# Self-attention values multiplied by high and low parts, with a triangle of value differences

## The chip, the cores and the metric

The program runs on one core of one Trainium2 chip. Its engines are TensorE (PE; its weight loads are the rows PEld), VectorE (DVE), ScalarE (ACT), GpSimd (POOL) and SyncE (SP), which starts most DMAs. Each engine works through its own queue of instructions in order and waits on semaphores. The metric is the device time of one launch in microseconds; less is better. Before the change it is 1614.92 us, the median of 3 runs (1614.67 to 1617.2).

## What is computed

One decoder layer on x of 4 x 512 x 512 in float32: a self-attention, a cross-attention, and a feed-forward with ternary weights. Only the self-attention and one side job of it (the mean of the absolute feed-forward weights) are touched:

```python
q = h @ wq_comp @ wq_up                       # 16 heads of 128
q = _rmsnorm(_apply_partial_rope(q, cos, sin), q_norm_w)
k = _rmsnorm(_apply_partial_rope(h @ wk, cos, sin), k_norm_w)
v = h @ wv                                    # one k and one v for all heads
mask = (diff >= 0) & (diff < WIN)             # WIN = 128, diff = query - key
probs = jax.nn.softmax(jnp.concatenate([scores, sink], axis=-1), axis=-1)
attn = jnp.einsum('bhts,bsd->bhtd', probs[..., :t], v)
...
scale = 1.0 / jnp.clip(jnp.mean(jnp.abs(w)), EPS)   # of each feed-forward weight
```

## The kernel before

The self-attention (phase_self_attention) takes the tokens in 16 tiles of 128 rows and the 16 heads in 4 groups of 4, so that there are 64 steps, step k being tile k // 4 and group k % 4. The window of 128 keys means that a query row sees keys of its own tile up to itself, and the keys behind them in the tile before. The first tile of each batch of four has its own tile only. The text calls its steps one-block steps (k = 0 to 3, 16 to 19, 32 to 35, 48 to 51) and the 48 others two-block steps.

A row of probabilities has just 128 live keys over both tiles. So copy_predicated (L547) lays the scores of both tiles over one another in 128 columns, the softmax runs on 128 columns, and the transposed probabilities ps_pT are parted again by two multiplications with 0/1 triangles: pT_own (L572) with the triangle of the own tile, pT_prev (L575) with the other. Two float32 matmuls, L729 and L732, multiply them with the values of the own tile and the tile before and add up in ps_a. Nearly all other matmuls of the phase are made by the helper three (L659 to L662): each operand is split into a high part rounded to float32r and a low part, and hi x hi, hi x lo and lo x hi are added up. The split costs one ACT copy (the high part) and one DVE subtraction (the low part).

The engines are software-pipelined by hand. In loop round c each engine does, in the order of its code:
- PE: scores of step c, values of step c - 2 (ps_a), transposition of q of step c + 1 (L742), transposition of the probabilities of step c - 1 (L754), up-projection of step c + 3, now and then work on a new tile (transposition of h when c % 4 is 1, the k/v/q projection when c % 4 is 2, transposition of k when c % 4 is 0), and the output product of step c - 3 (12 matmuls).
- DVE: copy_predicated and maximum of step c, neg_max (L553), aT_lo of c - 2, neg_r (L563), qT_lo of c + 1, pT_own and pT_prev of c - 1, the sum q_ss of c + 2, f_part (L585, the sum of absolute feed-forward weights, in rounds 0 to 23) and at the end inv_den of step c, the reciprocal at L602.
- ACT: aT_hi of c - 2 (L447), qT_hi of c + 1 (L451), the four exponentials of step c (L458), sink_exp (L461), the quantisation of a feed-forward chunk (L442 and L467, rounds 24 to 47), h (L474, when c % 4 is 0), and the copy q of c + 3 (L481). qcT_hi and kT_hi (L431, L434) of a new tile stand at the start of rounds with c % 4 of 1.
- POOL: squares and rotary embedding of q of step c + 2 (L629 and rotate, L613 to L617), the same for k of a new tile when c % 4 is 3, sink_arg (L643), den (L647), the multiplication of the probabilities by inv_den (L650), and q_r of c + 2 (L655).

PE may start the scores of c + 1 only when the exponentials of step c have read ps_s. There is no planner: the code's order is the order of the queues.

## Time and profile before

| | before |
|---|---|
| median of 3 runs | 1614.92 us (1614.67 to 1617.2) |
| the profiled execution, its own time | 1617.68 us |
| its span, first to last instruction | 1615.8 us |
| PE busy | 1549.0 us, 96% |
| DVE, ACT, POOL busy | 1228.1, 1186.8, 1267.7 us |
| self-attention steps | about 73 us to 588 us |

The profiled execution lies 2.8 us above the median. The page gives busy time for each engine, and the span in 40 slices of 40.4 us with the busy share in tenths; self-attention ends in the 15th slice. The granted TensorE clock is 1.00 throughout from 120 to 560 us. The columns of a timeline row are start, duration, engine, line, operation, output and inputs, and in brackets the engine's idle time before it and what ended it. Rows overlap where the next instruction starts before the last has ended, so the cost of one in a chain is the distance of two starts.

### The profile page before, as it was taken

What the parts mean: (1) busy time and instruction counts of PE and PEld (TensorE: products, weight loads), DVE (VectorE), ACT (ScalarE), POOL (GpSimd) and SP (SyncE); (2) the same over time, 40 slices, a digit from 0 to 9 for tenths busy, and PEclk for the clock granted to TensorE, in tenths of its full rate; (3) what the DMA queues carried; (4) which work ended last, traced back from release to release, by engine and by line L of the source; (5) the groups of instructions that cost most, each with busy time, mean ns of one, the idle gap of its engine ahead of it and who ended that gap; (6) DMA issues with size and microseconds to landing.
All of it is one profiled execution on the core that took longest, in us unless ns stands there. A gap on an engine that the chain in (4) does not pass through costs nothing. (4 is left out here: it accounts for less than half of the span.)

```text
span 1615.8 us, 23949 instructions
## 1 busy us (share of the span) xinstructions
PE 1549.0 (96%) x7520; PEld 1072.6 (66%) x7520; DVE 1228.1 (76%) x2242; ACT 1186.8 (73%) x1962; POOL 1267.7 (78%) x1141
## 2 busy tenths in 40 slices
PE   8999999999999988999999999999999978999996
PEld 3577787787788756666666666766666536666664
DVE  2489989878877756788978888788888666767773
ACT  2454556778755435999999889989998937878875
POOL 0487787787787724999999999999999949988850
...
DMA packets 57191, 110.24 MB, mean 68 GB/s; under 512 B 9245, under 2 KB 13597, under 8 KB 56683
## 3 DMA queue, kind: packets, MB, share of 16 engines
...
q8 instruction: 62, 1.02, 0.3%
q10 hardware_dynamic: 1578, 1.07, 0.2%
...
## 5 line engine op out<-in xcount | busy, mean ns | idle before, releaser
L1443 POOL TENSOR_TENSOR x_p_lo<-x_p,x_p_hi 128x1024 fp32r<-128x1024 f32 x255 | 603.0, 2397 | 59.3 <-ACT x_p_hi L1209 34.4
L1345 DVE TENSOR_REDUCE x_maxes<-x_ps_a 128x1 f32<-128x1024 f32 x252 | 306.9, 1218 | 114.4 <-PE x_ps_a L1544 110.7
L1172 ACT ACTIVATE x_p<-x_ps_b,x_any_valid 128x1024 f32<-128x1024 f32 x256 | 284.8, 1113 | 55.8 <-PE x_ps_b L1524 49.7
L1209 ACT ACTIVATE x_p_hi<-x_p 128x1024 fp32r<-128x1024 f32 x256 | 271.2, 1060 | 6.3
L1524 PE MATMUL x_ps_b<-x_Q,x_K 103*128 103x512 f32 x512 | 218.9, 509 | 12.1 <-ACT x_p L1172 10.0
L1584 PE MATMUL x_ps_o<-x_p_hi,x_V 128*96 128x512 f32 x512 | 208.6, 407 | 2.7 <-POOL x_p_lo L1443 2.1
L1585 PE MATMUL x_ps_o<-x_p_lo,x_V 128*96 128x512 f32 x512 | 201.3, 393 | 0.0
L1544 PE MATMUL x_ps_a<-x_K,x_Q 99*128 99x512 f32 x504 | 164.5, 407 | 4.7 <-POOL x_Q L1431 2.8
L1524 PEld LDWEIGHTS x_ps_b<-x_Q,x_K 103*128 103x128 f32 x512 | 87.5, 191 | 106.3 <-issue 58.8
L447 ACT ACTIVATE a_aT_hi<-a_ps_a 128x512 fp32r<-128x512 f32 x64 | 38.3, 598 | 153.8 <-PE a_ps_a L732 124.2
L458 ACT ACTIVATE a_work<-a_ps_s,a_neg_max,a_q_r 128x128 f32<-128x128 f32 x256 | 113.9, 464 | 7.9 <-DVE a_neg_max L553 7.7
L1544 PEld LDWEIGHTS x_ps_a<-x_K,x_Q 99*128 99x128 f32 x504 | 90.5, 190 | 40.4 <-DVE x_maxes L1345 16.5
L650 POOL TENSOR_TENSOR a_work<-a_work,a_inv_den 128x512 f32<-128x512 f32 x64 | 67.7, 1057 | 58.7 <-DVE a_inv_den L602 58.7
L1584 PEld LDWEIGHTS x_ps_o<-x_p_hi,x_V 128*96 128x96 f32 x512 | 82.7, 161 | 43.5 <-POOL x_p_lo L1443 5.4
L660 PE MATMUL a_ps_out<-a_w_hi,a_aT_hi 128*128 128x512 f32 x256 | 104.5, 408 | 0.0
L1585 PEld LDWEIGHTS x_ps_o<-x_p_lo,x_V 128*96 128x96 f32 x512 | 83.0, 162 | 30.2
L661 PE MATMUL a_ps_out<-a_w_lo,a_aT_hi 128*128 128x512 f32 x256 | 101.3, 396 | 0.0
L662 PE MATMUL a_ps_out<-a_w_hi,a_aT_lo 128*128 128x512 f32 x256 | 101.1, 395 | 0.0
L629 POOL TENSOR_TENSOR a_work<-a_q 128x512 f32<-128x512 f32 x64 | 66.4, 1037 | 16.0 <-ACT a_q L481 16.0
L661 PE MATMUL a_ps_s<-a_kT_lo,a_qT_hi 128*128 128x256 f32 (+1 forms) x256 | 72.3, 282 | 0.0
L662 PE MATMUL a_ps_s<-a_kT_hi,a_qT_lo 128*128 128x256 f32 (+1 forms) x256 | 72.0, 281 | 0.0
L1984 PE MATMUL f_ps_u<-shared,f_hqT 128*128 128x512 bf16 x256 | 67.3, 386 | 4.6 <-DVE f_f L1928 4.6
...
## 6 DMA issues: line engine op xcount, KB each, us to landing
...
```

Source lines behind the costliest of these rows:

```text
L458: act.activation(p[:, c % 2, j, :], ps_s[:, j, 0:P], ACT.Exp, scale=q_r[:, c % 4, j:j + 1], bias=neg_max[:, c % 2, j:j + 1], accum_out=row ...
L660: pe.matmul(out_ap, hi, rhs_hi, start=start, stop=False)
L661: pe.matmul(out_ap, hi, rhs_lo, start=False, stop=False)
L662: return pe.matmul(out_ap, lo, rhs_hi, start=False, stop=stop)
L1172: act.activation(p[:, v % 3, :, :], ps_b[:, :, :], ACT.Exp, scale=any_valid[:, b % 2:b % 2 + 1]).then_inc(exp_ready, 1)
L1209: act.activation(p_hi[:, r], p[:, v % 3], ACT.Copy).then_inc(hi_ready, 1)
L1345: dve.tensor_reduce(out=maxes[:, c % 2, 3 + r:4 + r], in_=scores_bank(n)[:, :, :], axis=mybir.AxisListType.XY, op=ALU.max).then_inc(max_re ...
L1443: pool.tensor_tensor(out=p_lo[:, v % 3, blocks], in0=p[:, v % 3, blocks], in1=p_hi[:, r, blocks].bitcast(F32), op=ALU.subtract)\
L1524: last = pe.matmul(ps_b[:, j, :], K[0:ROWS + 7, g, kb * P:(kb + 1) * P], Q[0:ROWS + 7, hh, :], start=True, stop=True)
L1544: last = pe.matmul(scores_bank(n)[:, j, :], Q[0:ROWS + 3, h2, r * P:(r + 1) * P], K[0:ROWS + 3, g2, j * 512:(j + 1) * 512], start=True, st ...
L1584: pe.matmul(bank[0:ROWS, :], vs, p_hi[:, rw, j], start=(rw == 0 and j == 0), stop=False)
L1585: last = pe.matmul(bank[0:ROWS, :], vs, p_lo[:, w % 3, j], start=False, stop=(rw == 3 and j == 1))
```

## The change

The values v, and the difference dv of the values of the tile before and the own tile, are split into high and low parts. The probabilities ps_pT are no longer masked for the own tile: all of them are multiplied with the own tile's v, and the part of the other triangle is multiplied with dv = v(before) - v(own), which corrects it. Both products are done by three, so each step has 3 or 6 float32r matmuls where it had 1 or 2 float32 ones.

For this ACT makes pT_hi (a copy, ahead of the exponentials of the same round), DVE makes pT_lo, pT_prev_hi and pT_prev_lo (3 instructions where 2 were; pT_own is gone), and per tile ACT makes v_hi and dv_hi, POOL dv, v_lo and dv_lo. On DVE the three stand behind the sum q_ss and just ahead of the reciprocal; pT_own and pT_prev stood ahead of q_ss. The sum of absolute weights f_part moves from DVE (tensor_reduce) to ACT (Abs with an accumulated output), in the same rounds.

```diff
         def _(act):
...
+                if 0 <= c - 1 < STEPS:
+                    k = c - 1
+                    act.wait_ge(pT_made, k + 1)
+                    if k:
+                        act.wait_ge(a_made, k)
+                    act.activation(pT_hi[:, :], ps_pT[:, :], ACT.Copy).then_inc(pT_hi_ready, 1)
                 if 0 <= c < STEPS:
                     act.wait_ge(neg_max_ready, 4 * c + 4)
...
+                t = tile_of(c, 1)
+                if t is not None:
+                    act.wait_ge(v_ready, t + 1)
+                    if t >= 2:
+                        act.wait_ge(a_made, 4 * (t - 1))
+                    act.activation(v_hi[:, t % 2, :], v[:, t % 3, :], ACT.Copy).then_inc(v_hi_ready, 1)
+                t = tile_of(c, 0)
+                if t is not None and t % TPB:
+                    act.wait_ge(dv_ready, two_block_tiles(t + 1))
+                    act.activation(dv_hi[:, t % 2, :], dv[:, :], ACT.Copy).then_inc(dv_hi_ready, 1)
+                if 0 <= c < FFN_CHUNKS:
+                    act.wait_ge(f_abs_in[c % 4], 16 * (c // 4 + 1))
+                    act.activation(f_abs[:, c % 4, :], f_abs[:, c % 4, :], ACT.Abs, accum_out=f_part[:, c:c + 1]).then_inc(f_part_ready, 1)
...
         def _(dve):
...
-                    dve.tensor_tensor(out=pT_own[:, :].rearrange("p (a b) -> p a b", a=G1), in0=ps_pT[:, :].rearrange("p (a b) -> p a b", a=G1),
-                                      in1=own_part, op=ALU.mult).then_inc(pT_own_ready, 1)
-                    if len(blocks(k // 4)) == 2:
-                        dve.tensor_tensor(out=pT_prev[:, :].rearrange("p (a b) -> p a b", a=G1), in0=ps_pT[:, :].rearrange("p (a b) -> p a b", a=G1),
-                                          in1=prev_part, op=ALU.mult).then_inc(pT_prev_ready, 1)
...
-                    if 0 <= c < FFN_CHUNKS:
-                        dve.wait_ge(f_abs_in[c % 4], 16 * (c // 4 + 1))
-                        dve.tensor_reduce(out=f_part[:, c:c + 1], in_=f_abs[:, c % 4, :], axis=AXX, op=ALU.add,
-                                          apply_absolute_value=True).then_inc(f_part_ready, 1)
...
+                    dve.wait_ge(pT_hi_ready, k + 1)
+                    if k:
+                        dve.wait_ge(a_made, k)
+                    dve.tensor_tensor(out=pT_lo[:, :], in0=ps_pT[:, :], in1=pT_hi[:, :].bitcast(F32), op=ALU.subtract).then_inc(pT_lo_ready, 1)
+                    if len(blocks(k // 4)) == 2:
+                        dve.tensor_tensor(out=pT_prev_hi[:, :].rearrange("p (a b) -> p a b", a=G1), in0=ps_pT[:, :].rearrange("p (a b) -> p a b", a=G1),
+                                          in1=prev_part, op=ALU.mult).then_inc(pT_prev_hi_ready, 1)
+                        dve.wait_ge(pT_lo_ready, k + 1)
+                        dve.tensor_tensor(out=pT_prev_lo[:, :].rearrange("p (a b) -> p a b", a=G1),
+                                          in0=pT_lo[:, :].bitcast(F32).rearrange("p (a b) -> p a b", a=G1),
+                                          in1=prev_part, op=ALU.mult).then_inc(pT_prev_lo_ready, 1)
                 if 0 <= c < STEPS:
                     dve.wait_ge(den_ready, c + 1)
...
         def _(pool):
...
+                t = tile_of(c, 1)
+                if t is not None:
+                    if t % TPB:
+                        pool.wait_ge(v_ready, t + 1)
+                        if two_block_tiles(t):
+                            pool.wait_ge(dv_lo_ready, two_block_tiles(t))
+                        pool.tensor_tensor(out=dv[:, :], in0=v[:, (t - 1) % 3, :], in1=v[:, t % 3, :], op=ALU.subtract).then_inc(dv_ready, 1)
+                    pool.wait_ge(v_hi_ready, t + 1)
...
+                t = tile_of(c, 0)
+                if t is not None and t % TPB:
+                    pool.wait_ge(dv_hi_ready, two_block_tiles(t + 1))
...
         def _(pe):
...
-                    last = pe.matmul(ps_a[:, :], v[:, blk[-1], :], pT_own[:, :], start=True, stop=len(blk) == 1)
+                    if k % 4 == 0:
+                        pe.wait_ge(v_lo_ready, t + 1)
+                    last = three(ps_a[:, :], v_hi[:, t % 2, :], v_lo[:, t % 2, :], pT_hi[:, :], pT_lo[:, :], True, len(blk) == 1)
                     if len(blk) == 2:
...
-                        last = pe.matmul(ps_a[:, :], v[:, blk[0], :], pT_prev[:, :], start=False, stop=True)
+                        pe.wait_ge(pT_prev_lo_ready, two_blocks(k + 1))
+                        last = three(ps_a[:, :], dv_hi[:, t % 2, :], dv_lo[:, t % 2, :], pT_prev_hi[:, :], pT_prev_lo[:, :], False, True)
```

v shrinks from four tiles to a ring of three (in the buffer work), so ACT's copy into it (L420) waits for v_lo of two tiles back and the last dv instead of for the products.

The order on DVE in a two-block round of a later tile, before, from neg_max to the reciprocal:

```order
L553 TENSOR_SCALAR a_neg_max<-a_s_max,a_neg_r,a_neg_sinks 128x1 x4
L558 TENSOR_TENSOR a_aT_lo<-a_ps_a,a_aT_hi 128x512
L563 TENSOR_SCALAR a_neg_r<-a_q_r 128x4
L565 TENSOR_TENSOR a_qT_lo<-a_ps_qT,a_qT_hi 128x512
L572 TENSOR_TENSOR a_pT_own<-a_ps_pT,a_window 128x512
L575 TENSOR_TENSOR a_pT_prev<-a_ps_pT,a_window 128x512
L580 TENSOR_REDUCE a_q_ss<-a_work 128x4
L582 TENSOR_SCALAR a_q_ss<-a_q_ss 128x4
L602 RECIPROCAL a_inv_den<-a_den 128x4
```

The same place of the changed kernel (its line numbers are larger):

```order
L587 TENSOR_SCALAR a_neg_max<-a_s_max,a_neg_r,a_neg_sinks 128x1 x4
L592 TENSOR_TENSOR a_aT_lo<-a_ps_a,a_aT_hi 128x512
L597 TENSOR_SCALAR a_neg_r<-a_q_r 128x4
L599 TENSOR_TENSOR a_qT_lo<-a_ps_qT,a_qT_hi 128x512
L604 TENSOR_REDUCE a_q_ss<-a_work 128x4
L606 TENSOR_SCALAR a_q_ss<-a_q_ss 128x4
L625 TENSOR_TENSOR a_pT_lo<-a_ps_pT,a_pT_hi 128x512
L627 TENSOR_TENSOR a_pT_prev_hi<-a_ps_pT,a_window 128x512
L630 TENSOR_TENSOR a_pT_prev_lo<-a_pT_lo,a_window 128x512
L635 RECIPROCAL a_inv_den<-a_den 128x4
```

The work on the transposed probabilities went behind the sum and has one instruction more, and the reciprocal stays last.

The order on ACT from the exponentials of a round with c % 4 of 0 (c = 12, while the feed-forward weights are summed) to kT_hi of the next round, before:

```order
L458 ACTIVATE a_work,a_row_sum<-a_ps_s,a_neg_max,a_q_r 128x128 x4
L461 ACTIVATE a_sink_exp<-a_sink_arg 128x4
L474 ACTIVATE shared<-a_xt,a_ln_bias,a_ln_rstd 128x512
L481 ACTIVATE a_q<-a_ps_up 128x512
L431 ACTIVATE a_qcT_hi<-a_ps_front 128x128
L434 ACTIVATE a_kT_hi<-a_ps_front 128x128
```

The same place of the changed kernel, from pT_hi:

```order
L472 ACTIVATE a_pT_hi<-a_ps_pT 128x512
L479 ACTIVATE a_work,a_row_sum<-a_ps_s,a_neg_max,a_q_r 128x128 x4
L482 ACTIVATE a_sink_exp<-a_sink_arg 128x4
L492 ACTIVATE a_dv_hi<-a_work 128x128
L495 ACTIVATE shared,a_f_part<-shared 128x1024
L508 ACTIVATE shared<-a_xt,a_ln_bias,a_ln_rstd 128x512
L515 ACTIVATE a_q<-a_ps_up 128x512
L446 ACTIVATE a_qcT_hi<-a_ps_front 128x128
L449 ACTIVATE a_kT_hi<-a_ps_front 128x128
```

dv_hi and the sum of absolute weights now stand between sink_exp and kT_hi, and pT_hi stands ahead of the exponentials.

## Rows read from the trace of the kernel before

**Rows 1.** The page: busy time of the engines, and their tenths in 40 slices

```profile
PE 1549.0 (96%) x7520; PEld 1072.6 (66%) x7520; DVE 1228.1 (76%) x2242; ACT 1186.8 (73%) x1962; POOL 1267.7 (78%) x1141
...
PE   8999999999999988999999999999999978999996
```

**Rows 2.** Stretches of the self-attention: busy time by engine, granted clock, DMA share

```profile
120.00:260.00 140.00, 140.00 (x756) 112.45 (x755) 129.16 (x302) 73.14 (x252) 110.25 (x190) 1.00 0.35 81
260.00:460.00 200.00, 200.00 (x1079) 159.68 (x1078) 168.76 (x423) 151.58 (x398) 161.81 (x271) 1.00 0.36 106
```

**Rows 3.** PE timeline of round 59 (two blocks), then of round 34 (one block)

```profile
541.85 1.02 PE L729 MATMUL a_ps_a<-a_pT_own,a_v 128*128 128x512 f32 x2
542.71 1.02 PE L732 MATMUL a_ps_a<-a_pT_prev,a_v 128*128 128x512 f32 x2
543.57 0.60 PE L742 MATMUL a_ps_qT<-ident,a_q 128*128 128x128 f32 x4
544.01 0.60 PE L754 MATMUL a_ps_pT<-ident,a_work 128*128 128x128 f32 x4
544.36 0.48 PE L660 MATMUL a_ps_up<-a_up_hi,a_qcT_hi 128*128 128x512 f32 x1
...
545.38 0.39 PE L661 MATMUL a_ps_out<-a_w_lo,a_aT_hi 128*128 128x512 f32 x1
545.61 0.39 PE L662 MATMUL a_ps_out<-a_w_hi,a_aT_lo 128*128 128x512 f32 x1
...
343.70 1.07 PE L729 MATMUL a_ps_a<-a_pT_own,a_v 128*128 128x512 f32 x2
344.61 0.60 PE L742 MATMUL a_ps_qT<-ident,a_q 128*128 128x128 f32 x4
```

**Rows 4.** DVE timeline: the reciprocals of rounds 18, 22, 34, 38 and 42

```profile
221.02 0.17 DVE L602 RECIPROCAL a_inv_den<-a_den 128x4 f32<-128x4 f32 x1
...
253.23 0.16 DVE L602 RECIPROCAL a_inv_den<-a_den 128x4 f32<-128x4 f32 x1
...
348.69 0.17 DVE L602 RECIPROCAL a_inv_den<-a_den 128x4 f32<-128x4 f32 x1
...
379.66 0.17 DVE L602 RECIPROCAL a_inv_den<-a_den 128x4 f32<-128x4 f32 x1
...
412.44 0.17 DVE L602 RECIPROCAL a_inv_den<-a_den 128x4 f32<-128x4 f32 x1
```

**Rows 5.** Who waited for whom, whole phase: us in total, times, longest

```profile
POOL a_work L650 <- DVE a_inv_den L602: 58.7, 64, 2.6
...
ACT a_sink_exp L461 <- POOL a_sink_arg L643: 33.5, 32, 2.6
```

**Rows 6.** ACT and DVE timelines from round 44 into round 45

```profile
428.06 1.17 ACT L467 ACTIVATE shared<-shared,a_f_clip 128x1024 bf16<-128x1024 f32 x1
429.10 0.83 ACT L474 ACTIVATE shared<-a_xt,a_ln_bias,a_ln_rstd 128x512 f32<-128x512 f32 x1
...
435.62 0.23 ACT L458 ACTIVATION_READ_ACCUMULATOR a_work<-a_ps_s,a_neg_max,a_q_r 128x1 f32 x1
...
430.78 0.29 DVE L528 TENSOR_TENSOR a_qcT_lo<-a_ps_front,a_qcT_hi 128x128 fp32r<-128x128 f32 x1 [1.03 <-ACT a_kT_hi L434]
```

**Rows 7.** Groups of instructions by form: busy us, mean ns, idle before

```profile
L585 DVE TENSOR_REDUCE a_f_part<-shared 128x1 f32<-128x1024 f32 x24 | 29.0, 1210 | 0.0
...
L575 DVE TENSOR_TENSOR a_pT_prev<-a_ps_pT,a_window 128x512 f32<-128x512 f32 x48 | 32.5, 677 | 0.0
...
L614 POOL TENSOR_TENSOR a_q_t<-a_q,a_rope 128x128 f32<-128x128 f32 x64 | 29.4, 459 | 0.0
...
L451 ACT ACTIVATE a_qT_hi<-a_ps_qT 128x512 fp32r<-128x512 f32 x64 | 38.0, 593 | 2.4 <-PE a_ps_qT L742 2.4
```

**Rows 8.** Two lines of DVE by themselves (min/median/max ns), and POOL beside the second

```profile
L563 DVE TENSOR_SCALAR a_neg_r<-a_q_r x64: 158/279/742, 69.9 to 566.9; 128x4 f32<-128x4 f32 x64
...
1286.61 3.78 DVE L1373 TENSOR_TENSOR x_p_lo<-x_p,x_p_hi 128x1024 fp32r<-128x1024 f32 x1 [7.53 <-ACT x_p_hi L1209]
...
1284.60 4.71 POOL L1443 TENSOR_TENSOR x_p_lo<-x_p,x_p_hi 128x1024 fp32r<-128x1024 f32 x2
```

More of the change, by code:

```diff
@@ L194, in phase_self_attention @@
         kT_lo = sb("kT_lo", [P, TPB * P], F32R)
[L195 removed]
+        v_hi = sb("v_hi", [P, 2, P], F32R)
+        v_lo = sb("v_lo", [P, 2, P], F32R)
+        dv_hi = sb("dv_hi", [P, 2, P], F32R)
+        dv_lo = sb("dv_lo", [P, 2, P], F32R)
         q = sb("q", [P, 2, G1, P])
[L197 removed]
         q_ss = sb("q_ss", [P, 2, G1])
```

47 lines of the change are left out of this document (29 added, 18 removed).

## Prediction

> **What bounds the kernel now.** I read the page first: PE is busy 96% of the span and at 9 tenths in nearly every slice of the self-attention [rows 1]. The stretches say the same more sharply: from 120 to 460 us PE has no idle time at all, at a granted clock of 1.00 [rows 2]. So PE sets the pace of the rounds, and shorter PE work shortens them, until something else does. The same rows show that the something else is near: DVE is busy 129.16 of 140 us up to 260 us, and POOL 161.81 of 200 after it. POOL's idle time, moreover, is mostly waiting: 58.7 us for the reciprocal in 64 rounds, and ACT waited for POOL's sink_arg in 32 of them [rows 5]. That is a ring, POOL to ACT to POOL to DVE to POOL. I therefore price the change twice, on PE, and on that ring.
>
> **The change on PE.** A float32 value matmul costs 0.86 us from start to start (541.85 to 542.71, 542.71 to 543.57), 0.91 in a one-block round (343.70 to 344.61) [rows 3]. A float32r matmul of 512 columns costs 0.23 (545.38 to 545.61), so three cost 0.70. The transposition behind the values takes 0.44 (543.57 to 544.01), and the next one, which does not follow a float32 product, 0.35 [rows 3]; I take 0.08 of that as gained too. A two-block round thus gains 2 x 0.16 + 0.08 = 0.40 us, a one-block round 0.16 to 0.21 + 0.08, say 0.25. Sum: 48 x 0.40 + 16 x 0.25 = 23.2 us, if nothing else binds; without the 0.08 it is 18. The worst bound is that no float32r matmul overlaps the next, as the single duration of 0.39 [rows 3] would have it, which loses 0.3 per product; the start-to-start distances speak against it.
>
> **The change on the ring.** Follow it over four rounds, from the reciprocal of one round with c % 4 of 2 to that of the next. The reciprocal releases POOL's multiplication; POOL then works without a gap through q_r, the squares, the rotation and, at c % 4 of 3, k's rotation, to sink_arg; ACT's sink_exp, den and the reciprocal follow, then POOL's round again up to sink_exp of c % 4 = 0. Then ACT has to get through its tail to kT_hi, for which DVE sat idle 1.03 us even before [rows 6], and DVE runs two rounds nearly without idling. Before, these four rounds took 253.23 - 221.02 = 32.2 us and 379.66 - 348.69 = 31.0 us where the one-block rounds had let PE run fast, that is, where the ring decided; where PE decided they took 412.44 - 379.66 = 32.8 [rows 4]. The change moves PE's 32.8 to 32.8 - 4 x 0.40 = 31.2. On the ring it adds:
> - POOL: dv and v_lo, 128x128 each like L614, 0.46 us busy and some 0.42 start to start: +0.84 [rows 7]. dv_lo runs beside DVE's rounds and is hidden by them.
> - ACT: dv_hi, +0.2 (a quarter of the columns of L451's 0.59, bounds 0.15 and 0.3) [rows 7]. In rounds 0 to 23 also the absolute sum: ACT's pass over 128x1024 is 1.04 from start to start (428.06 to 429.10) [rows 6], with an accumulator read 1.15.
> - DVE, in each of its two rounds: 3 instructions for 2 of 0.60 (0.677 busy) [rows 7], +0.6, so +1.2. In rounds 0 to 23 f_part's 1.21 [rows 7] goes, 1.13 start to start, in those two rounds and some 0.9 of it ahead of the third reciprocal: -3.2.
> - The port of POOL. pT_prev_lo is the first DVE operation of this phase's rounds with both large inputs in SBUF. What one costs beside POOL is seen at 1286.61: 3.78 us for 128x1024, ending when POOL's two had ended and its own pass was done [rows 8]. The tiny L563 takes 158 to 742 ns for the same 4 columns [rows 8], long when POOL is in the middle of an instruction. So I price pT_prev_lo from 0.6 (nobody in the way) to 0.6 + 1.0 (a whole L650 to wait for), and POOL's next instruction from 0 to 0.6 late. It mostly runs while POOL waits for the reciprocal behind it, where it costs POOL nothing; at c % 4 of 3 or 0 POOL is late and they meet. I take +0.6 per four rounds.
>
> By the Trainium skill, page "SBUF — State Buffer", section "Who interferes with whom", a DVE instruction with two SBUF inputs and a POOL instruction that reads SBUF exclude each other for the whole of the first one. The trace agrees with it in the 3.78 us of [rows 8]; by it all 48 pT_prev_lo could meet POOL, which is the slower rival below.
>
> The ring sums to: up to round 24, 32.2 + 0.84 + 0.2 + 1.15 - 3.2 + 1.2 + 0.6 = 33.0; in rounds 25 to 47, 31.0 + 0.84 + 0.2 + 1.2 + 0.6 = 33.8; behind them, without the quantisation's 1.04 on ACT and 0.4 on DVE, about 32.2. Compare with PE's 32.8 before and 31.2 after: in most of the phase the ring binds, and takes the gain.
>
> **What hides, and what the ring may be late by.** pT_hi (0.48 start to start) on ACT stands ahead of the exponentials, but values and transpositions come 0.3 earlier; the next scores start at 437.60, 1.8 us after the exponentials of round 45 ended (435.62 + 0.23) [rows 6], and 0.4 + 0.2 of that goes. So the ring can be some 1.2 us late before PE feels it, and 1.9 more behind one-block rounds, whose DVE work lacks copy_predicated and two pT instructions. The accumulation of f_part on ACT can wait for the same loads as before; the loads lead by two rounds and add nothing. The waits for v's ring of three are for work of a round or more ago: 0. No table load is added for Abs in the order of the program.
>
> **The sum by stretches** (after minus before; rounds counted from one c % 4 = 2 to the next):
> - ramp, rounds 0 to 5: DVE loses f_part, which the first rounds wait for; -1.0.
> - rounds 6 to 25: five groups, 33.0 against 32.8 in the two-block ones, the first with 1 us of slack in hand, one-block ones 0.6 better: -1.1.
> - rounds 26 to 49: 3 groups at 33.8 - 32.9 = +0.9, the one-block pair +0.2 and +0.7, the last, half without quantisation, -0.9: +2.7.
> - rounds 50 to 63: PE's pace again, 14 rounds at 0.25 to 0.40, with a little lost at 54: -4.6.
>
> Together -4.0. The profiled execution's 1617.68 becomes 1613.7; against the median, 2.8 lower, **1611**. Nothing behind the phase changes; what is gained ahead of its end carries over one to one.
>
> **Rivals.**
> 1. PE keeps the pace. If POOL and DVE absorb the additions (dv and v_lo under the reciprocal's wait of 0.9 us per round [rows 5], pT_prev_lo never meeting POOL), most of 23 us comes: -13 to -23, so 1592 to 1602. For it: POOL idles 38 of 200 us and DVE 31 [rows 2]. Against it: the ring's 31.0 and 32.2 us.
> 2. The port decides and the time ends slower. If pT_prev_lo meets POOL in every two-block round, DVE waits 0.4 (half of an average POOL instruction) in its two rounds on the ring and POOL 0.6 in its two: +2.0 per group in place of +0.6. Nine groups with 1.4 more each is +12.6: 1611 + 12 = 1623. It decides from the point where the ring exceeds PE's old 32.8, which it does already.
> 3. The float32r products don't gain (0.28 to 0.30 each beside fresh weights): PE is then unchanged, and the additions hide less: 1615 to 1618.
>
> **How the numbers follow.** Chances: my forecast, 1605 to 1616, 0.42; PE's pace, 0.28; the port, 1617 to 1630, 0.23; no gain on PE, 0.07. The likeliest case's own range is 1605 to 1616. For 8 in 10 the range reaches from 1594 into rival 1 to 1622 into rival 2. About 0.2% (3.2 us) is what a measurement of this kernel can tell from no change. Faster by more (under 1611.7): 0.28 + 0.21 of my case = 0.49. Within it: 0.21 + 0.06 = 0.27. Slower: 0.24.
>
> **What would show it.** On PE: value triples at 0.70 and rounds of 7.13 us behind round 56, in any case. Rounds 36 to 47: PE idle ahead of the scores, released by ACT's exponentials, or ahead of the up-projection, released by kT_lo, near c % 4 of 1 and 2; without such idling rival 1 has it. pT_prev_lo: a median near 0.68 with a tail to 1.3; a median near 1 is rival 2. Reciprocals four rounds apart: 33.8. I am wrong on the ring if these read 31.2, and on DVE if the reciprocal no longer ends POOL's waits. PE's idling could also lower the granted clock, which was 1.00 here [rows 2]; that would add to the slow side.

## The result, and the profile after the change

The changed kernel takes 1623.83 us (median of five runs, 1619.61 to 1624.43). The ratio to the kernel before is 1.0040, with a 95% interval of 1.0025 to 1.0054: slower by 0.4%, where 0.25% faster was forecast, and the time lies above the range of 1594 to 1622. The 1614.92 us from which the prediction started is at the low end for the kernel before: beside the experiments its medians were 1616.6 to 1617.6 us. So the ratios below, each with the 95% interval, say more than differences of medians taken at different times.

Busy time of the engines, from the page of the changed kernel, against [rows 1]:

```profile
PE 1535.3 (95%) x7599; PEld 1087.2 (67%) x7632; DVE 1235.5 (76%) x2266; ACT 1249.0 (77%) x2102; POOL 1293.4 (80%) x1181
```

PE has 14 us less work than before, DVE 7 more, ACT 62 more and POOL 26 more. What that does shows in the stretches of the self-attention, in the columns of [rows 2], with one more stretch behind them:

```profile
120.00:260.00 140.00, 136.45 (x777) 116.17 (x777) 117.74 (x293) 98.50 (x305) 113.78 (x194) 1.00 0.32 81
260.00:460.00 200.00, 193.15 (x1093) 162.82 (x1092) 177.75 (x433) 163.93 (x432) 166.64 (x278) 1.00 0.35 105
460.00:560.00 100.00, 99.50 (x573) 85.16 (x572) 84.22 (x206) 61.09 (x201) 85.69 (x144) 1.00 0.17 59
```

Before, PE was busy for the whole of both stretches; now it idles 3.6 and 6.9 us in them. PE itself became faster, as forecast in kind. Its timeline in round 58:

```profile
539.62 0.39 PE L708 MATMUL a_ps_a<-a_pT_hi,a_v_hi 128*128 128x512 f32 x1
539.86 0.39 PE L709 MATMUL a_ps_a<-a_pT_lo,a_v_hi 128*128 128x512 f32 x1
540.09 0.40 PE L710 MATMUL a_ps_a<-a_pT_hi,a_v_lo 128*128 128x512 f32 x1
540.79 0.47 PE L708 MATMUL a_ps_a<-a_pT_prev_hi,a_dv_hi 128*128 128x512 f32 x1 [0.30 <-DVE a_pT_prev_lo L630]
541.10 0.39 PE L709 MATMUL a_ps_a<-a_pT_prev_lo,a_dv_hi 128*128 128x512 f32 x1
541.33 0.40 PE L710 MATMUL a_ps_a<-a_pT_prev_hi,a_dv_lo 128*128 128x512 f32 x1
541.57 0.60 PE L795 MATMUL a_ps_qT<-ident,a_q 128*128 128x128 f32 x4
542.00 0.60 PE L807 MATMUL a_ps_pT<-ident,a_work 128*128 128x128 f32 x4
```

A product of three float32r matmuls takes 0.70 (539.62 + 3 x 0.23) where the float32 one took 0.86 [rows 3]; the second one here takes 0.78, since its first matmul comes behind a wait. The transposition behind it still takes 0.43. The 0.30 in brackets is new: PE waits for the last part that DVE makes.

Who waits for whom in the self-attention (us in total, times, longest), against [rows 5]:

```profile
ACT a_sink_exp L482 <- POOL a_sink_arg L676: 71.9, 50, 3.0
ACT a_aT_hi L462 <- PE a_ps_a L710: 53.9, 35, 3.6
POOL a_work L683 <- DVE a_inv_den L635: 50.4, 64, 2.3
POOL a_den L680 <- ACT a_sink_exp L482: 27.5, 64, 1.9
DVE a_inv_den L635 <- POOL a_den L680: 23.6, 24, 2.1
DVE a_qcT_lo L562 <- ACT a_kT_hi L449: 18.6, 15, 2.3
...
PE a_ps_up L708 <- DVE a_kT_lo L565: 6.2, 9, 1.0
PE a_ps_pT L807 <- POOL a_work L683: 5.1, 10, 1.5
PE a_ps_s L763 <- ACT a_work L479: 3.6, 3, 2.3
```

ACT's wait for sink_arg has doubled (33.5 us in 32 rounds before), and DVE waits 23.6 us for POOL's den, ahead of the reciprocal, where it waited 4.1 us before. The last three rows are the largest waits of PE itself. One turn of the ring, at the end of round 43 (c % 4 of 3), on POOL, ACT and DVE:

```profile
426.95 0.32 POOL L646 TENSOR_TENSOR shared<-shared,a_rope 128x64 f32<-128x64 f32 x1
...
428.58 0.83 POOL L672 TENSOR_TENSOR shared<-shared,a_qk_w 128x128 f32<-128x128 f32 x1
429.38 0.20 POOL L676 TENSOR_TENSOR a_sink_arg<-a_neg_max,a_sinks 128x4 f32<-128x4 f32 x1
429.89 0.20 POOL L680 TENSOR_TENSOR a_den<-a_row_sum,a_sink_exp 128x4 f32<-128x4 f32 x1 [0.32 <-ACT a_sink_exp L482]
430.38 1.04 POOL L683 TENSOR_TENSOR a_work<-a_work,a_inv_den 128x512 f32<-128x512 f32 x1 [0.29 <-DVE a_inv_den L635]
```

```profile
426.67 0.21 ACT L479 ACTIVATION_READ_ACCUMULATOR a_work<-a_ps_s,a_neg_max,a_q_r 128x1 f32 x1
429.61 0.20 ACT L482 ACTIVATE a_sink_exp<-a_sink_arg 128x4 f32<-128x4 f32 x1 [2.73 <-POOL a_sink_arg L676]
429.72 0.29 ACT L488 ACTIVATE a_v_hi<-a_work 128x128 fp32r<-128x128 f32 x1
429.92 1.14 ACT L501 ACTIVATE shared<-shared,a_f_clip 128x1024 bf16<-128x1024 f32 x1
430.96 0.57 ACT L515 ACTIVATE a_q<-a_ps_up 128x512 f32<-128x512 f32 x1
```

```profile
430.12 0.18 DVE L635 RECIPROCAL a_inv_den<-a_den 128x4 f32<-128x4 f32 x1 [1.03 <-POOL a_den L680]
```

The exponentials end at 426.88. POOL is by then in the rotations of q and k and comes to sink_arg 2.5 us later; ACT idles 2.73 us, and its ReLU, its copy of q and all that follows are late by that.

Where the phase lost its time, by the start of the first score matmul of a round in the two profiled runs (after minus before): +0.1 us at round 6, +2.9 at 26, +6.4 at 50, +5.4 at 63. In the whole span the profiled runs differ by only 1.9 us, since the rest of the program had a higher granted clock in this run of the changed kernel (0.994 on average over the span, against 0.990); its other four runs took 1622.3 to 1624.4 us at 0.992. (The clock also differed inside the ramp, 0.93 before and 0.96 changed from 73 to 120 us; from 120 to 560 us it was 1.00 in both.) Against a kernel before of 1616.7 us the ratio of 1.0040 is 6.5 us, and the phase's 5.4 is most of it.

### The profile page after: what moved, and what is told of

Read it like the earlier page. It is cut to its first block and busy times, and to the rows that moved or that the text cites. A ratio compares the mean times of both kernels' runs of the same rounds, so it can differ in the third digit from the quotient of the medians.

```text
span 1617.8 us, 24457 instructions
## 1 busy us (share of the span) xinstructions
PE 1535.3 (95%) x7599; PEld 1087.2 (67%) x7632; DVE 1235.5 (76%) x2266; ACT 1249.0 (77%) x2102; POOL 1293.4 (80%) x1181
## 5 line engine op out<-in xcount | busy, mean ns | idle before, releaser
L708 PE MATMUL a_ps_s<-a_kT_hi,a_qT_hi 128*128 128x256 f32 (+1 forms) x256 | 72.0, 281 | 1.5 <-ACT a_work L479 1.5
```

The costliest lines, as they stand in the source:

```text
L708: pe.matmul(out_ap, hi, rhs_hi, start=start, stop=False)
```

## The experiments

All are edits of the changed kernel, but for the last. The ratio is to the kernel before; the changed kernel stands at 1.0040. Where an expectation names a value of c % 4 for ACT's or POOL's waits, it counts by the round that PE is in, one ahead of the instruction's own for the sink's exponential, den and the reciprocal.

### Does the ring bind, or PE?

**PE's products put back to float32**, nothing else changed:

```diff
-last = three(ps_a[:, :], v_hi[:, t % 2, :], v_lo[:, t % 2, :], pT_hi[:, :], pT_lo[:, :], True, len(blk) == 1)
+last = pe.matmul(ps_a[:, :], v_hi[:, t % 2, :].bitcast(F32), pT_hi[:, :].bitcast(F32), start=True, stop=len(blk) == 1)
```

> The changed kernel with its two float32r triples on PE put back as one float32 product each, v_hi x pT_hi and dv_hi x pT_prev_hi (the low parts are still made on all engines, but not used, so the result lacks their share). PE's round is as long as before the change, all other engines' work is that of the changed kernel. Theory 1 (the ring of POOL, ACT and DVE binds in rounds 6 to 49, where four rounds take 33.6 to 34.1 us against 32.9 of PE's old pace): only the rounds with PE's pace lose, 14 at the end x 0.33 and the ramp, so 1624 + 4 to 8 = 1628 to 1632. Theory 2 (PE still sets the pace and something else stalls it now and then): all 48 x 0.33 + 16 x 0.15 = 18 us come back, 1642.

Measured: 1627.52 us, ratio 1.0061 (1.0049 to 1.0073). That is half a microsecond below theory 1 and 14 below theory 2: in this kernel PE's saving is worth 0.2%, 3.4 us, and not 18. In rounds 26 to 49 the phase took 4.4 us more than before, against 3.5 in the changed kernel. The ring binds.

**All that was added beside PE taken out** (pT_prev_lo, dv, v_lo and dv_lo, and all but 8 columns of the absolute sum):

```diff
-in0=pT_lo[:, :].bitcast(F32).rearrange("p (a b) -> p a b", a=G1),
-in1=prev_part, op=ALU.mult).then_inc(pT_prev_lo_ready, 1)
...
-pool.tensor_tensor(out=dv[:, :], in0=v[:, (t - 1) % 3, :], in1=v[:, t % 3, :], op=ALU.subtract)
-pool.tensor_tensor(out=v_lo[:, t % 2, :], in0=v[:, t % 3, :], in1=v_hi[:, t % 2, :].bitcast(F32), op=ALU.subtract)
-pool.tensor_tensor(out=dv_lo[:, t % 2, :], in0=dv[:, :], in1=dv_hi[:, t % 2, :].bitcast(F32), op=ALU.subtract)
...
-act.activation(f_abs[:, c % 4, :], f_abs[:, c % 4, :], ACT.Abs, accum_out=f_part[:, c:c + 1])
+act.activation(f_abs[:, c % 4, 0:8], f_abs[:, c % 4, 0:8], ACT.Abs, accum_out=f_part[:, c:c + 1])
```

> The changed kernel without what it adds beside PE: no pT_prev_lo (PE uses pT_prev_hi in its place), no dv, v_lo and dv_lo on POOL (PE uses v_hi and dv_hi in their place, dv_hi is a copy of v), and the absolute sum over 8 of its 1024 columns; the result is not the reference's in these parts. PE's work is that of the changed kernel. Theory 1 (ring): PE's pace of 7.20 per two-block and 6.68 per one-block round in nearly all of the phase, so 16 to 20 us below the kernel before, 1595 to 1599. Rival (PE's product triples save less than the rows say, or the granted clock falls when PE idles less evenly): 1608 or more.

Measured: 1598.87 us, ratio 0.9885 (0.9873 to 0.9898). Here the whole saving arrives, and PE is busy without a gap again, in the stretches from 120 and from 260 us of this kernel:

```profile
120.00:260.00 140.00, 140.00 (x817) 122.17 (x816) 111.60 (x294) 88.17 (x319) 115.27 (x198) 1.00 0.34 81
260.00:460.00 200.00, 200.00 (x1166) 174.22 (x1165) 172.64 (x431) 168.85 (x449) 165.52 (x274) 1.00 0.35 106
```

Its two-block rounds without tile work take 7.21 us against 7.53, its one-block rounds 6.41 against 6.57: 0.32 and 0.16 per round. Four rounds take 31.6 us, against 32.9 before and 33.6 to 34.1 in the changed kernel.

### What each addition costs

**pT_prev_lo read from PSUM**, of the same size, but without a second large SBUF input:

```diff
-in0=pT_lo[:, :].bitcast(F32).rearrange("p (a b) -> p a b", a=G1),
+in0=ps_pT[:, :].rearrange("p (a b) -> p a b", a=G1),
```

> The changed kernel with pT_prev_lo made from ps_pT in PSUM instead of from pT_lo in SBUF (it holds a wrong part then, which falsifies the result a little); DVE has the same number of instructions of the same size, but none with two large SBUF inputs. Theory of the port (POOL's instructions that meet pT_prev_lo are stretched or held, some 1.4 us per group of four rounds over nine groups): 1611 to 1613. Theory of plain additions (the ring is late from the count of instructions; only two or three small POOL instructions per group are held 0.4 each): 1618 to 1622. If the port does nothing: 1623 to 1625.

Measured: 1616.08 us, ratio 0.9991 (0.9977 to 1.0005): a gain of 0.5%, between the theory of the port (1611 to 1613) and that of plain additions (1618 to 1622). The port costs that, but mostly not on DVE. By line (min/median/max ns), pT_prev_lo, sink_arg and den of the changed kernel:

```profile
L630 DVE TENSOR_TENSOR a_pT_prev_lo<-a_pT_lo,a_window x48: 672/676/989, 116.1 to 584.8; 128x512 fp32r<-128x512 f32 x48
L676 POOL TENSOR_TENSOR a_sink_arg<-a_neg_max,a_sinks x64: 188/199/654, 76.1 to 578.5; 128x4 f32<-128x4 f32 x64
L680 POOL TENSOR_TENSOR a_den<-a_row_sum,a_sink_exp x64: 198/200/664, 77.9 to 580.6; 128x4 f32<-128x4 f32 x64
```

and of this one:

```profile
L630 DVE TENSOR_TENSOR a_pT_prev_lo<-a_ps_pT,a_window x48: 671/675/684, 118.1 to 580.9; 128x512 fp32r<-128x512 f32 x48
L676 POOL TENSOR_TENSOR a_sink_arg<-a_neg_max,a_sinks x64: 196/201/211, 75.6 to 574.7; 128x4 f32<-128x4 f32 x64
L680 POOL TENSOR_TENSOR a_den<-a_row_sum,a_sink_exp x64: 199/201/207, 77.4 to 576.7; 128x4 f32<-128x4 f32 x64
```

With pT_lo from SBUF, POOL's two smallest instructions are held up to 0.46 us each, and both stand on the ring. It happens to sink_arg in 4 rounds and to den in 10, 5.5 us in sum, each time beside a pT_prev_lo. The last product of k's rotation (L672, 128x128) is held too, to 0.83 us in 6 tiles and 0.55 in 4, where it takes 0.46 by itself. Without it neither of the small ones ever takes over 0.21. The long tail of pT_prev_lo is gone too, and behind round 56 all of PE's waits: rounds 50 to 63 gain 3.1 us against the kernel before, in place of 1.0.

**pT_prev_lo left out** (PE takes pT_prev_hi in its place):

```diff
-dve.tensor_tensor(out=pT_prev_lo[:, :].rearrange("p (a b) -> p a b", a=G1),
...
-last = three(ps_a[:, :], dv_hi[:, t % 2, :], dv_lo[:, t % 2, :], pT_prev_hi[:, :], pT_prev_lo[:, :], False, True)
+last = three(ps_a[:, :], dv_hi[:, t % 2, :], dv_lo[:, t % 2, :], pT_prev_hi[:, :], pT_prev_hi[:, :], False, True)
```

> The changed kernel without DVE's pT_prev_lo (PE uses pT_prev_hi in its place, so the low part's share is missing from the result). Made from PSUM, at the same duration on DVE, the ratio was 0.9991 against 1.0040, which is the price of the port. Theory of the ring: DVE's 0.6 us in its two rounds per group are on the ring too, up to 1.2 x 10 groups less: 0.992 to 0.994, 1603 to 1608. Rival: the duration itself is hidden and only the port counts: 0.998 to 1.000, 1613 to 1617.

Measured: 1607.43 us, ratio 0.9939 (0.9925 to 0.9953), another 0.5% below the version from PSUM: DVE's 0.6 us per round costs as much as the port. Rounds 10 to 13 take 31.92 us in place of 33.64.

**POOL's dv, v_lo and dv_lo left out** (v_hi and dv_hi in their place):

```diff
-pool.tensor_tensor(out=dv[:, :], in0=v[:, (t - 1) % 3, :], in1=v[:, t % 3, :], op=ALU.subtract)
-pool.tensor_tensor(out=v_lo[:, t % 2, :], in0=v[:, t % 3, :], in1=v_hi[:, t % 2, :].bitcast(F32), op=ALU.subtract)
-pool.tensor_tensor(out=dv_lo[:, t % 2, :], in0=dv[:, :], in1=dv_hi[:, t % 2, :].bitcast(F32), op=ALU.subtract)
...
-act.activation(dv_hi[:, t % 2, :], dv[:, :], ACT.Copy)
+act.activation(dv_hi[:, t % 2, :], v[:, (t - 1) % 3, :], ACT.Copy)
```

> The changed kernel without dv, v_lo and dv_lo on POOL: v_hi and dv_hi stand in for the low parts, and dv_hi is a copy of v, so the result is not the reference's. All else is as in the changed kernel, pT_prev_lo included. The prediction's term for them: 0.84 per group on the ring (dv_lo hidden), over nine to ten groups 8 us: 1615 to 1617. If dv_lo is on the ring as well: 1.26 per group, 1611 to 1613. Rival (POOL has room, the port alone decides): 1621 to 1625.

Measured: 1606.75 us, ratio 0.9939 (0.9924 to 0.9955): 1.0% for 40 instructions of 0.46 us, 18 us of busy time. Both gains that I had given (down to 1615 and to 1611) were too small. Rounds 10 to 13 take 32.39 us, 1.25 less, which is what three instructions of 0.42 come to; so dv_lo was most likely not hidden. No run takes it out alone.

**The absolute sum back on DVE:**

```diff
+dve.tensor_reduce(out=f_part[:, c:c + 1], in_=f_abs[:, c % 4, :], axis=AXX, op=ALU.add, apply_absolute_value=True)
-act.activation(f_abs[:, c % 4, :], f_abs[:, c % 4, :], ACT.Abs, accum_out=f_part[:, c:c + 1])
```

> The changed kernel with f_part's sum of absolute values back on DVE, where it stood before the change, in rounds 0 to 23. Theory as in the prediction (the sum's move took 3.2 us off DVE's part of the ring per four rounds and put 1.15 on ACT's): +2 per group over five groups, 1631 to 1635. Rival (up to round 25 ACT's tail ahead of kT_hi and the up-projection's copy is what is late, and DVE has the room): ACT gets 1.15 us per group back, 1618 to 1621.

Measured: 1629.24 us, ratio 1.0070 (1.0056 to 1.0083). Moving the sum did help, by 0.3%. But in rounds 10 to 13 it is 1.2 us (34.86 against 33.64), not 2.05, and over rounds 6 to 25 1.3 per four rounds.

**The absolute sum over 8 columns on ACT:**

```diff
-act.activation(f_abs[:, c % 4, :], f_abs[:, c % 4, :], ACT.Abs, accum_out=f_part[:, c:c + 1])
+act.activation(f_abs[:, c % 4, 0:8], f_abs[:, c % 4, 0:8], ACT.Abs, accum_out=f_part[:, c:c + 1])
```

> The changed kernel with ACT's absolute sum over 8 of its 1024 columns, which falsifies the quantisation's scale; all else as in the changed kernel. It prices ACT's share of the moved sum. The prediction's term: 1.15 us per group on the ring, five groups up to round 25: 0.9965 to 1.000 as the ratio to the kernel before (1.0040 with the whole sum), 1612 to 1617. With the sum back on DVE the same stretch was 6.7 us longer than in the changed kernel; if DVE is what is late there, and not ACT, a shorter sum on ACT gives nothing: 1.003 to 1.005, 1621 to 1625.

Measured: 1617.18 us, ratio 1.0008 (0.9996 to 1.0020); rounds 10 to 13 take 32.72 us, 0.92 less. So ACT's share is 0.9 here, near the 1.15 of the prediction (over all of rounds 6 to 25 it is 0.6 per four rounds); and what leaving DVE brought is some 1.2 + 0.9 = 2.1, not 3.2, if the two add up.

### Does the order matter?

**DVE's three parts ahead of q_ss**, where the masked products stood before:

```diff
+dve.tensor_tensor(out=pT_lo[:, :], in0=ps_pT[:, :], in1=pT_hi[:, :].bitcast(F32), op=ALU.subtract)
...
 dve.tensor_reduce(out=q_ss[:, k % 2, :], in_=q_sq[:, :, :], axis=AXX, op=ALU.add)
...
-dve.tensor_tensor(out=pT_lo[:, :], in0=ps_pT[:, :], in1=pT_hi[:, :].bitcast(F32), op=ALU.subtract)
```

> The changed kernel with DVE's pT_lo, pT_prev_hi and pT_prev_lo put back to where the products with the masks stood before the change, ahead of q_ss. Theory of the ring: DVE's work up to the reciprocal is the same in sum, and PE and POOL wait for neither of the moved results in rounds 6 to 49, so nothing changes there; behind round 56 PE no longer waits 0.30 for pT_prev_lo: 1.002 to 1.004, 1619 to 1624. Theory of the port: pT_prev_lo no longer stands beside POOL's sink_arg and den (0.20 us each, 0.58 to 0.65 beside it), but beside the rotation, whose instructions it holds 0.6 at a time: 1.003 to 1.008, 1621 to 1630; or it frees den and sink_arg as pT_prev_lo from PSUM did: 0.999 to 1.001, 1615 to 1619.

Measured: 1621.60 us, ratio 1.0032 (1.0020 to 1.0043). The new place on DVE costs nothing that these runs separate from the changed kernel. That is the theory of the ring. Behind round 56 PE no longer waits for pT_prev_lo, twice 0.3 us before, but once 0.66 us for POOL's product, so rounds 56 to 62 take 51.0 us against 51.3.

**The reciprocal ahead of pT_prev_lo:**

```diff
+dve.reciprocal(inv_den[:, c % 2, :], den[:, c % 2, :]).then_inc(inv_ready, 1)
 dve.tensor_tensor(out=pT_prev_lo[:, :].rearrange("p (a b) -> p a b", a=G1),
...
-dve.reciprocal(inv_den[:, c % 2, :], den[:, c % 2, :]).then_inc(inv_ready, 1)
```

> The changed kernel with DVE's reciprocal ahead of pT_prev_lo instead of behind it. Theory of the ring without the port: POOL waits 1.2 to 1.5 us for the reciprocal at c % 4 of 2 and 3, gets it 0.6 earlier there, and a group is 0.6 to 1.2 shorter: 1613 to 1619. Theory of the port: pT_prev_lo now starts when POOL starts its multiplication of p, which has all its large operands in SBUF; one of them is held for the length of the other, and the 0.6 comes back on POOL or as a pT_prev_lo of over 1 us on DVE: 1621 to 1630.

Measured: 1619.10 us, ratio 1.0013 (1.0003 to 1.0022), between the two expectations: most of the earlier reciprocal is lost again in POOL's multiplication, which pT_prev_lo now meets nearly every time (by line, this kernel):

```profile
L686 POOL TENSOR_TENSOR a_work<-a_work,a_inv_den x64: 1040/1397/1402, 77.9 to 579.3; 128x512 f32<-128x512 f32 x64
```

It took 1.04 in the changed kernel. pT_prev_lo (0.66 us here) starts 0.16 us ahead of it and runs beside it for 0.50, and 0.36 are added to it. By the Trainium skill, "SBUF — State Buffer", section "Who interferes with whom", a DVE instruction with two SBUF inputs and a POOL instruction that reads SBUF exclude each other. This and the rows of sink_arg and den agree with it in kind, not in full: 0.50 us side by side cost 0.36.

**ACT's absolute sum and ReLU ahead of the sink's exponential**, into ACT's wait for sink_arg:

```diff
+act.activation(f_abs[:, c % 4, :], f_abs[:, c % 4, :], ACT.Abs, accum_out=f_part[:, c:c + 1])
+act.activation(f_quant[:, k % 4, :], f_raw[:, k % 2, :], ACT.Relu, scale=-1.0, bias=f_clip[:, :])
 act.wait_ge(sink_arg_ready, c + 1)
 act.activation(sink_exp[:, c % 2, :], sink_arg[:, c % 2, :], ACT.Exp)
...
-act.activation(f_abs[:, c % 4, :], f_abs[:, c % 4, :], ACT.Abs, accum_out=f_part[:, c:c + 1])
-act.activation(f_quant[:, k % 4, :], f_raw[:, k % 2, :], ACT.Relu, scale=-1.0, bias=f_clip[:, :])
```

> The changed kernel with ACT's absolute sum and the quantisation's ReLU moved from behind the sink's exponential to between the exponentials and the wait for POOL's sink_arg. In the changed kernel ACT waits there 2.0 to 2.4 us in rounds with c % 4 of 0, 0.9 at 1, 0.7 at 2 and none at 3. Theory of the ring: at c % 4 of 0 the 1.04 to 1.15 us fit into the wait, and qcT_hi, kT_hi and the up-projection's copy come that much earlier, which DVE and PE wait for at c % 4 of 1; 0.5 to 1.1 per group over ten groups: 1613 to 1619. Rival: at c % 4 of 3 and 2 the sink's exponential comes up to 1.1 later and holds POOL's den and the reciprocal, which are on the ring too: 1621 to 1628.

Measured: 1614.96 us, ratio 0.9988 (0.9979 to 0.9996), as the theory of the ring had it. ACT's wait for sink_arg in the round of c = 43 falls from 2.73 to 1.71 us. (By ACT's own c the waits of the changed kernel are 2.73, 1.00, 0 and 0.87 us at c = 43, 40, 41 and 42; the last two stand the other way round in the expectation.)

**POOL's dv and v_lo between den and the wait for the reciprocal:**

```diff
+pool.tensor_tensor(out=dv[:, :], in0=v[:, (t - 1) % 3, :], in1=v[:, t % 3, :], op=ALU.subtract)
+pool.tensor_tensor(out=v_lo[:, t % 2, :], in0=v[:, t % 3, :], in1=v_hi[:, t % 2, :].bitcast(F32), op=ALU.subtract)
 pool.wait_ge(inv_ready, c + 1)
...
 pool.tensor_tensor(out=q_r[:, k % 4, :], in0=q_ss[:, k % 2, :], in1=half_neg[:, :], op=ALU.pow)
-pool.tensor_tensor(out=dv[:, :], in0=v[:, (t - 1) % 3, :], in1=v[:, t % 3, :], op=ALU.subtract)
-pool.tensor_tensor(out=v_lo[:, t % 2, :], in0=v[:, t % 3, :], in1=v_hi[:, t % 2, :].bitcast(F32), op=ALU.subtract)
```

> The changed kernel with POOL's dv and v_lo (at c % 4 of 3) moved from behind q_r to between den and the wait for the reciprocal. Theory of the ring: they fit into that wait of 1.2 us, 0.8 per group is gone from POOL's part: 1615 to 1618. Rival: they run there beside DVE's pT_prev_lo, and either holds the other, so that the reciprocal or they come later: 1622 to 1626.

Measured: 1615.87 us, ratio 0.9990 (0.9976 to 1.0004). The time is the one forecast, but the reason given was not the right one. The wait of 1.3 us is that for the reciprocal of c % 4 of 2; for those of c % 4 of 3, where dv and v_lo went, POOL waits only 0.29 us in the changed kernel, and that is all that they fill. Nor does pT_prev_lo leave the ring alone: the next sink_arg, which it held for 0.45 us, is free, but the den behind it now takes 0.58 in place of 0.20. So it stays open where most of the 0.88 us that rounds 10 to 13 gain come from.

**Both moves together**, and **with the reciprocal ahead of pT_prev_lo as well:**

> Both moves of order together (ACT's absolute sum and ReLU ahead of the wait for sink_arg; POOL's dv and v_lo ahead of the wait for the reciprocal). Alone they gave ratios of 0.9988 and 0.9990 to the kernel before, against 1.0040 of the changed kernel. Theory: both shorten the same ring at different places, so they add while PE can follow (its own pace would give about 0.9885): 0.994, 1607 to 1610. Rival: each takes the same slack (ACT's sink exponential is late at c % 4 of 3, where POOL's moved instructions stand): 0.997 to 0.999, 1612 to 1616.

> The two moves of order and DVE's reciprocal ahead of pT_prev_lo. Alone the last gave 1.0013, with POOL's multiplication stretched from 1.05 to 1.31 us by pT_prev_lo, which then runs beside it. Theory: the reciprocal's 0.6 us less 0.26 of the stretch adds to the other two where POOL waits: 0.992, 1602 to 1607. Rival: PE waits more for the later pT_prev_lo (0.2 to 0.4 us in a few rounds behind one-block rounds even alone), and there is no gain over the two moves: 0.994 to 0.998, 1607 to 1613.

Measured: 1610.33 us, ratio 0.9952 (0.9940 to 0.9965), and 1610.93 us, ratio 0.9961 (0.9949 to 0.9973). Alone the two moves gave 0.5% each, together 0.9%, so within the intervals they add; the third brings nothing on top.

**The triangle's parts without two SBUF inputs:** DVE masks ps_pT in place in PSUM, ACT copies pT_prev_hi behind the sink's exponential, and DVE subtracts behind the reciprocal; both moves of order are in it.

```diff
-dve.tensor_tensor(out=pT_prev_hi[:, :].rearrange("p (a b) -> p a b", a=G1),
+dve.tensor_tensor(out=ps_pT[:, :].rearrange("p (a b) -> p a b", a=G1),
                   in0=ps_pT[:, :].rearrange("p (a b) -> p a b", a=G1), in1=prev_part, op=ALU.mult)
...
+act.activation(pT_prev_hi[:, :], ps_pT[:, :], ACT.Copy).then_inc(pT_prev_hi_ready, 1)
...
+dve.tensor_tensor(out=pT_prev_lo[:, :], in0=ps_pT[:, :], in1=pT_prev_hi[:, :].bitcast(F32), op=ALU.subtract)
```

> The two moves of order, and the triangle's parts made without an instruction of two large SBUF inputs: DVE multiplies ps_pT by the mask in place in PSUM, ACT copies it to pT_prev_hi behind the sink's exponential, and DVE subtracts (pT_prev_lo) behind the reciprocal. Same result as the reference's. Theory of the port: the 0.5% that pT_prev_lo from PSUM gave alone comes on top of the two moves, less ACT's copy of 0.48 us where ACT's tail is on the ring (c % 4 of 0): 0.990 to 0.993, 1601 to 1606. Rival: ACT, now at 1249 + 23 us busy, has its up-projection copy late by 0.48 in every two-block round, and PE waits for it or for pT_prev_lo behind it: 0.996 to 1.003, 1610 to 1621.

Measured: 1629.53 us, ratio 1.0080 (1.0067 to 1.0093), 1.3% above the same kernel without this edit, and above both expectations. The port is free (POOL's den never takes over 0.21 us), but there is a new link from DVE to ACT and back, and PE waits for its end. Its 15.2 us, in the rows below, are most of the 19 us; POOL's wait for ACT's sink's exponential also grew, from 29.7 to 54.7 us, and no run parts the two. The waits of this kernel:

```profile
DVE a_pT_prev_lo L645 <- ACT a_pT_prev_hi L500: 21.7, 42, 0.6
...
PE a_ps_a L729 <- DVE a_pT_prev_lo L645: 15.2, 23, 1.1
```

### Where the ring can be cut

The rows of round 43 point to sink_arg. Its input, neg_max, is there before the exponentials start, but it stood behind both rotations. In these versions the four instructions of a rotation can be called apart, and sink_arg stands behind the first product of q's rotation, with the rest of it and all of k's ahead of den (k_r and k_w, which move along, and the waits of k are left out):

```diff
-rotate(q[:, k % 2], q_t, (k // 4) % TPB, G1, q_mul_ready, 3 * k + 3, q_rope_ready)
+rotate(q[:, k % 2], q_t, (k // 4) % TPB, G1, q_mul_ready, 3 * k + 3, q_rope_ready, (0, 1, 2, 3) if c < 0 else (0,))
...
 pool.tensor_tensor(out=sink_arg[:, c % 2, :], in0=neg_max[:, c % 2, :], in1=sinks[:, G1 * g:G1 * g + G1],
                    op=ALU.add).then_inc(sink_arg_ready, 1)
+rotate(q[:, (c + 2) % 2], q_t, ((c + 2) // 4) % TPB, G1, q_mul_ready, 3 * (c + 2) + 3, q_rope_ready, (1, 2, 3))
+t = tile_of(c, 5)
+if t is not None:
+    rotate(qck[:, P:].unsqueeze(1), k_t[:, :, :].unsqueeze(1), t % TPB, 1, k_mul_ready, 3 * t + 3, k_rope_ready)
...
 pool.wait_ge(sink_exp_ready, c + 1)
```

**With both moves of order:**

> On top of the two moves of order (0.9952): POOL's sink_arg directly behind the first product of the rotation, and the rest of q's rotation and k's rotation behind it, ahead of den. POOL does the same work, but gives ACT its sink_arg before the exponentials end instead of up to 2 us after. Theory: at c % 4 of 3 and 0 the sink's exponential, den and the reciprocal come 1 to 1.6 us earlier (DVE idles 1.0 and ACT 1.6 there, PE waits 0.9 to 1.0 for POOL's product), so the group is that much shorter: 0.991 to 0.993, 1602 to 1606. Rival: POOL's whole stream is as long as before, den only moves from behind one wait to behind another, and the product of p comes no earlier: 0.994 to 0.996, 1607 to 1611; with k_hat late for ACT 1612 or more.

**With the move on POOL alone:**

> As the kernel with POOL's sink_arg moved forward, but with ACT's absolute sum and ReLU where the changed kernel has them, behind the sink's exponential. Since sink_arg is now there when the exponentials end, their place ahead of it may cost den up to 1.1 us. Theory: DVE reaches the reciprocal later than den in either order, and only ACT's tail at c % 4 of 0 counts, which is 1.1 longer here: 0.3% above the other order, 1606 to 1612. Rival: den decides, this order is the better one: 1600 to 1604.

**With neither, sink_arg alone:**

> The changed kernel with POOL's sink_arg moved forward alone (behind the first product of the rotation; the rest of q's and k's rotation follows it, ahead of den); dv and v_lo stay behind q_r. With dv and v_lo ahead of the wait for the reciprocal as well the ratio was 0.9902. Theory: sink_arg's place is the cause, and the rest is small: 0.990 to 0.993, 1600 to 1605. Rival: the places of dv and v_lo give their own 0.5% here too, 0.994 to 0.996, 1607 to 1611.

Measured, in this order: 1603.55 us, ratio 0.9919 (0.9906 to 0.9932); 1600.82 us, 0.9902 (0.9889 to 0.9914); 1603.94 us, 0.9923 (0.9910 to 0.9935). So one instruction's place is worth 1.2% (1.0040 to 0.9923). The first had ACT's sum and ReLU ahead of the sink's exponential, where they now only delay it. The second beats both kernels, by 1.0 and 1.4%. Its waits:

```profile
ACT a_aT_hi L462 <- PE a_ps_a L734: 108.1, 57, 4.6
POOL a_work L707 <- DVE a_inv_den L635: 49.3, 50, 2.8
DVE a_inv_den L635 <- POOL a_den L694: 16.4, 21, 2.8
```

The 71.9 us of ACT's wait for sink_arg are gone, and ACT waits for PE again. The same place as above, round 43, on POOL and then ACT of this kernel:

```profile
408.10 0.20 POOL L680 TENSOR_TENSOR a_sink_arg<-a_neg_max,a_sinks 128x4 f32<-128x4 f32 x1
...
411.54 0.84 POOL L691 TENSOR_TENSOR shared<-shared,a_qk_w 128x128 f32<-128x128 f32 x1
412.33 0.21 POOL L694 TENSOR_TENSOR a_den<-a_row_sum,a_sink_exp 128x4 f32<-128x4 f32 x1
```

```profile
410.24 0.24 ACT L479 ACTIVATION_READ_ACCUMULATOR a_work<-a_ps_s,a_neg_max,a_q_r 128x1 f32 x1
410.33 0.24 ACT L482 ACTIVATE a_sink_exp<-a_sink_arg 128x4 f32<-128x4 f32 x1
```

The sink's exponential follows the last exponential directly, and POOL's rotations run meanwhile. POOL does the same work as before; den comes when its own stream allows.

**The kernel before with sink_arg in the new place:**

> The kernel before the change with POOL's sink_arg moved forward in the same way. It divides 0.9902 between the order and the change. Theory (PE set the pace before, so the order gives only what the ring cost: the ramp and a few late scores, up to 3 us): 0.998 to 1.001, 1613 to 1618. Rival (the order alone brings the gain, and the change nothing even then): 0.990 to 0.994, 1600 to 1607.

Measured: 1614.94 us, ratio 0.9990 (0.9981 to 0.9999). From the start of round 6 to that of round 63 it takes what the kernel before took, less 0.16 us; the other 1.8 us that it is ahead by then stem from the ramp. In the kernel before, PE hid the late sink_arg nearly wholly; in the changed kernel it is what decides. With it moved, the change is worth 0.9923 / 0.9990, 0.7%, and 0.9% with dv and v_lo moved too.

## Why the prediction was wrong

**What failed is the pricing of the ring.** Two terms of the sum did it: the credit of 3.2 us per four rounds for taking f_part off DVE (the runs give 2.1), and "PE's pace again" with -4.6 us for rounds 50 to 63, where the ring and the port bind too (-1.0 measured). Both are worked out below.

**That the ring would bind and PE would not was right.** PE's saving is real (0.9885 when nothing else binds) and is worth 0.2% in the changed kernel. Most signs named ahead came: triples of 0.70, PE idle ahead of the up-projection and of the scores, reciprocals of rounds 34, 38 and 42 at 33.7 us apart (33.8 forecast). PE's round of 7.13 us did not: it is 7.2 at best, and four rounds at PE's pace take 31.6 us, not 31.2. The reciprocals:

```profile
353.13 0.18 DVE L635 RECIPROCAL a_inv_den<-a_den 128x4 f32<-128x4 f32 x1
...
386.86 0.17 DVE L635 RECIPROCAL a_inv_den<-a_den 128x4 f32<-128x4 f32 x1
...
420.56 0.17 DVE L635 RECIPROCAL a_inv_den<-a_den 128x4 f32<-128x4 f32 x1
```

**The sum by stretches**, forecast and measured in the profiled runs:

| rounds | forecast | measured |
|---|---|---|
| 0 to 5 | -1.0 | +0.1 |
| 6 to 25 | -1.1 | +2.8 |
| 26 to 49 | +2.7 | +3.5 |
| 50 to 63 | -4.6 | -1.0 |
| sum | -4.0 | +5.4 |

- **Rounds 6 to 25: the credit for f_part on DVE.** I had it at -3.2 per four rounds, as if the whole ring had run through DVE in nearly three rounds. The runs give 2.1. The group came out at 33.64 us, not 33.0, which is some 3 of the 3.9 us missed there. The slack counted on did not help either: the first group, rounds 6 to 9, already takes 33.65 us against 33.03 before, and the one-block group, rounds 18 to 21, is 0.3 us longer and not 0.6 shorter. Two other terms of the same sum were off in opposite senses: POOL's values 1.25 in place of 0.84, where I had called dv_lo hidden; ACT's sum 0.92 in place of 1.15. dv_hi's 0.2 was in no run taken out. The DVE term of 1.2 and the port's 0.6 fit what the runs of pT_prev_lo give there (33.64 to 33.12 to 31.92: 0.5 for the port, 1.2 for the duration). These corrections come to about +1.2, where the group missed by +0.64: such prices, each taken off the finished ring, do not add up exactly.
- **Rounds 50 to 63: "PE's pace again".** PE's own gain there is 3.4 us, shown by the relieved kernel, not 4.6: the 0.08 per transposition did not come, and a product saves 0.16 as forecast. The other 2.4 were lost because the ring and the port bind there too; with pT_prev_lo from PSUM 3.1 us of the 3.4 arrive. I had counted the port only where the ring was already late.
- **Rounds 0 to 5.** The start of round 6 lay between 2.9 us before and 2.2 us behind that of the kernel before in the various kernels, without order. The granted clock of these rounds differed as well, from 0.92 to 1.00 between the profiled runs. The 1.0 there can't be judged, and differences of 0.2% or less between two of these kernels may be the ramp's.
- **The port (rival 2)** gave 1623 us, and that is the time, but by luck. It put the port at 2.0 us per group, 18 in all; measured it is 0.5 in rounds 10 to 13 and 0.5% in all, 8 us, near the 0.6 per group of my own sum. Its mechanism was half right: pT_prev_lo's median stayed at 0.68, its tail ended at 0.99 and not 1.3, and by the sign that I had set the rival was out. The cost sat on the other side of the port, in POOL's instructions of 0.20 us; I had named that half too, but gave no sign for it.
- **Rival 1 (PE's pace, 0.28)** needed POOL and DVE to absorb the additions. They can: nearly the same work in another order on POOL gives 0.9902. In this order they can't. **Rival 3** is refuted by the triples of 0.70.

What I left out altogether is that a ring is made of an order. I took the order on POOL as fixed, read 33.5 us of ACT waiting for sink_arg [rows 5], and priced additions to the ring, without asking what sink_arg stood behind.

The ramp, the sizes of the single terms in rounds 26 to 49, which overlap, and why about a seventh of PE's saving (0.9902 against 0.9885) is still missing in the best version stay open. By the traces, which leave out the ramp's scatter, it is 3.4 us of 16 from round 6 to 63, all but 0.1 of it ahead of round 50. POOL's den is still held there in 14 rounds, up to 0.75 us, so the port is a candidate; no run has the new order and pT_prev_lo from PSUM together.
